# One fused attention-and-FFN layer on one core: setup chunks 0 to 2 reordered on VectorE, TensorE and ScalarE, one high part moved to GpSimd, and the row transpose of x1 done as two transfers

## The reference, cut to what matters

```python
r = sigmoid(x @ Wr); k = x @ Wk; v = x @ Wv
state = decayed running sum over time of k * v     # per channel
y = rmsnorm(r * state, ln_w)
x = layernorm(x + y @ Wo)
h = gelu(x @ (alpha1 * sign(w1)).T + b1)           # 256 -> 1024
x = layernorm(x + h @ (alpha2 * sign(w2)).T + b2)  # 1024 -> 256
```

## Time and profile before

| | us |
|---|---|
| median of 3 runs (822.38 to 822.54) | 822.49 |
| the profiled execution | 822.86 |
| its span | 821.0 |
| TensorE products, busy | 798.2 (97%) |
| VectorE, busy | 772.6 (94%) |
| ScalarE, busy | 678.9 (83%) |
| GpSimd, busy | 295.6 (36%) |

### The profile page before, as it was taken

The page is one execution under the profiler, slowest core; times in us unless marked ns, Lnnn a source line. Parts: engine busy times, 40 slices in busy tenths (PEclk is TensorE's granted clock), DMA queues, the critical chain, the costliest instruction groups (busy, mean ns, idle before and its releaser), DMA issues.

```text
span 821.0 us, 16564 instructions
## 1 busy us (share of the span) xinstructions
PE 798.2 (97%) x5173; PEld 505.3 (62%) x5173; DVE 772.6 (94%) x1467; ACT 678.9 (83%) x971; POOL 295.6 (36%) x570
## 2 busy tenths in 40 slices
PE   6989999999999999999999999999999999999986
PEld 4555666656666656666656666665666665666653
DVE  7998999999999999999999999999999999999886
ACT  7887888888888888888888888888888888887775
POOL 3343323344323344233344333344332334332344
PEclk9999999999999999999999999999999999999999
DMA  8413554444553434554434554444455344444313
GB/s 249 91 46 78 129 113 94 102 103 102 128 128 83 110 88 102 128 128 92 113 80 109 118 128 103 102 90 108 109 128 112 93 98 106 102 102 103 78 33 97
DMA packets 169847, 86.27 MB, mean 105 GB/s; under 512 B 130145, under 2 KB 165473, under 8 KB 169825
## 3 DMA queue, kind: packets, MB, share of 16 engines
q1 hardware_dynamic: 148304, 52.97, 29.8%
q0 software_dynamic: 4608, 16.78, 10.8%
q10 hardware_dynamic: 16912, 16.26, 5.8%
HBM read 20.45 MB, written 16.78 MB: 45 GB/s over the span
## 4 chain that ended last, share of the span: by engine, by line
PE 89%; DVE 4%; POOL 2%; issue 2%; ACT 2%; DMA 1%; POOLq 0%; DVEq 0%; ACTq 0%; SPq 0%
PE ps_r L362 28%; PE ps_o L483 26%; PE ps_f L433 19%; PE ps_r L433 6%; PE ps_o L388 6%; PE ps_o L393 3%; DVE hid_lo L981 1%; DMA x_in<-in_L_attn_x_dram 1%; DVE u L932 1%; ACT hid L662 1%; DVE u_st L940 0%; PE ps_s L370 0%; POOL root L1284 0%; POOL y_sqs L1272 0%; ACT hid_hi L697 0%
## 5 line engine op out<-in xcount | busy, mean ns | idle before, releaser
L483 PE MATMUL ps_o<-w2T,hid_hi 128*128 128x256 f16 x992 | 218.9, 273 | 3.4 <-DVE hid_lo L981 3.0
L483 PE MATMUL ps_o<-w2T,hid_lo 128*128 128x256 f16 x992 | 218.8, 273 | 0.0
L362 PE MATMUL ps_r<-x_t,proj_hi 128*128 128x512 f16 x768 | 197.1, 379 | 1.7 <-DVE proj_lo L1057 1.2
L433 PE MATMUL ps_f<-x_t,w1T 128*128 128x512 f16 x768 | 181.7, 379 | 1.6 <-DVE x_t L965 1.3
L662 ACT ACTIVATE hid<-ps_f,b1c,f_scale 128x512 f32<-128x512 f32 x192 | 145.3, 774 | 41.6 <-PE ps_f L433 36.6
L981 DVE SCALAR_TENSOR_TENSOR hid_lo<-hid,hid_scale,hid_hi 128x1024 f16<-128x1024 f32 (+1 forms) x136 | 160.3, 1222 | 0.9 <-POOL hid_hi L1305 0.6
L1272 POOL TENSOR_TENSOR y_sqs<-y_sq 128x512 f32<-128x512 f32 x32 | 46.7, 1459 | 308.4 <-ACT y_sq L637 308.4
L362 PEld LDWEIGHTS ps_r<-x_t,proj_hi 128*128 128x128 f16 x768 | 74.5, 98 | 92.1 <-issue 3.4
L697 ACT ACTIVATE hid_hi<-hid,hid_scale 128x2048 f16<-128x2048 f32 (+2 forms) x72 | 128.0, 1778 | 3.2
L433 PEld LDWEIGHTS ps_f<-x_t,w1T 128*128 128x128 f16 x768 | 74.9, 98 | 79.6 <-issue 1.6
L362 PE MATMUL ps_r<-x_t,proj_lo 128*128 128x512 f16 x384 | 114.2, 379 | 0.0
(11 more groups left out here) (182 smaller groups left out, 1333.0 us busy)
## 6 DMA issues: line engine op xcount, KB each, us to landing
x_in<-in_L_attn_x_dram SPq DMA_DIRECT2D x32, 512.0 KB, 4.4
res<-b_row POOLq DMA_DIRECT2D x32, 512.0 KB, 4.6
out_dram<-res ACTq DMA_DIRECT2D x31, 512.0 KB, 3.1
w_in<-in_L_ffn_w_dram SPq DMA_DIRECT2D x2, 1024.0 KB, 10.2
x_t<-x_st SPq DMA_TRANSPOSE x59, 4.3
b_row<-in_L_ffn_b_dram SPq DMA_DIRECT2D x1, 512.0 KB, 13.2
proj_in<-in_L_attn_Wk_dram SPq DMA_DIRECT2D x1, 256.0 KB, 5.2
proj_in<-in_L_attn_Wv_dram SPq DMA_DIRECT2D x1, 256.0 KB, 5.4
```

The source lines that it names most:

```text
L362: last = nc.tensor.matmul(ps_r[:, m, :], w[:, m, dc, ec * P:(ec + 1) * P], xx[:, :, dc, :], start=(n == 0), stop=(n == 3 * DC - 1))
L433: last = nc.tensor.matmul(f1_bank[hc % NF], w1T[:, hc, dc, :], xx[:, :, dc, :], start=(dc == 0 and n == 0), stop=(dc == DC - 1 and n == 1))
L483: last = nc.tensor.matmul(o_tok[:, tt, :], hh[:, hc, tt * P:(tt + 1) * P], w2T[:, :, hc, :], start=(hc == 0 and n == 0), stop=(hc == HC - ...
```

## The change

- TensorE's prologue: T1(0) stands behind R(2)'s group ec=1, m=0 instead of m=1. F1(0) of tile 0 stands ahead of sum_wmax, which now also waits for take_bounds(1,3).
- VectorE's prologue: x1l(0) ahead of hidden_bound; block_sums(1) ahead of hidden_scale; scans(2,2,0) behind mean_sq(1); hl of pairs 0 and 1 behind ustats(1), then norm1(1), hl of pairs 2 and 3, x1l_rows(1), kvs(2,2,1), scans(2,2,1).
- ScalarE's prologue: alphas2 in two parts, one after the second r gate of chunk 2 (ahead of gelu of tile 0), the other after gelu of tile 2; the high part of pair 1 is left out; that of pair 3 ahead of x1h_rows(1).
- GpSimd: the high part of pair 1 (`hh_first`), the product that scales alpha2 (within `diagonal`), and the order unscales, diagonal, hh_first, root_u(1), x1b(0).
- SyncE: x1's transpose in every chunk is two transfers, the high half after x1h_rows and F1, the low half after x1l_rows. The semaphore x1t counts 32 instead of 16 for a chunk.

```diff
@@ sync
-            sp.sem_inc(s_x1t, 16)
+            sp.sem_inc(s_x1t, 32)
...
-            def transpose(dst, src):
-                return sp.dma_start(dst[:, :, :, :, :].rearrange("p s tt dc t -> p (s tt dc) t"),
-                                    src[:, :, :, :].rearrange("p s tt d -> p (s tt d)"), transpose=True)
+            def transpose(dst, src, parts=slice(0, 2)):
+                return sp.dma_start(dst[:, parts].rearrange("p s tt dc t -> p (s tt dc) t"),
+                                    src[:, parts].rearrange("p s tt d -> p (s tt d)"), transpose=True)
...
-                    sp.wait_ge(s_x1l, i + 2)
+                    sp.wait_ge(s_x1h, i + 2)
                     sp.wait_ge(s_f1, HC * i + HC)
                     sp.sem_inc(s_issued, 1)
-                    transpose(x1_t, x1_st).then_inc(s_x1t, 16)
+                    transpose(x1_t, x1_st, slice(0, 1)).then_inc(s_x1t, 16)
+                    sp.wait_ge(s_x1l, i + 2)
+                    sp.sem_inc(s_issued, 1)
+                    transpose(x1_t, x1_st, slice(1, 2)).then_inc(s_x1t, 16)
@@ tensor
-                    pe.wait_ge(s_x1t, 16 * c + 16)
+                    pe.wait_ge(s_x1t, 32 * c + 32)
...
-                R(2, False, looped=False, ecs=(1,), slot=2, ms=range(2))
+                R(2, False, looped=False, ecs=(1,), slot=2, ms=(0,))
                 T1(0, 0, True)
-                R(2, False, looped=False, ecs=(1,), slot=2, ms=(2,))
+                R(2, False, looped=False, ecs=(1,), slot=2, ms=range(1, 3))
                 pe.wait_ge(s_ms, 1)
-                sum_wmax(ps_wmax[:, 5:6], 5, 1, 6)
                 sum_bounds(1, NCH)
                 pe.wait_ge(s_w1T, 16)
-                F1(0, NCH, range(0, 3), gates=3)
+                F1(0, NCH, range(0, 1), gates=3)
+                pe.wait_ge(s_xtmp, 4)
+                sum_wmax(ps_wmax[:, 5:6], 5, 1, 6)
+                F1(0, NCH, range(1, 3), gates=3)
@@ scalar
-                act.wait_ge(s_x1t, 16 * c)
+                act.wait_ge(s_x1t, 32 * c)
...
-            def hh(c, part):
+            def hh(c, part, counted=0):
...
-                                     scale=hid_scale[:, :]).then_inc(s_hh, part.stop - part.start)
+                                     scale=hid_scale[:, :]).then_inc(s_hh, part.stop - part.start + counted)
...
                 r_gates(2, 2, (0,))
-                act.wait_ge(s_sgn2, 1)
-                alphas2()
                 x1h(0, 1)
                 ysq(1, (1,), y=y_second)
                 r_gates(2, 2, (1,))
+                alphas2((0,))
                 act.wait_ge(s_ready, 1)
                 gelu(0, range(0, 1))
                 yh(1, y_second)
                 gelu(0, range(1, 2))
                 act.wait_ge(s_ready, 2)
                 hh(0, pairs[0])
-                gelu(0, range(2, 4))
-                hh(0, pairs[1])
-                gelu(0, range(4, 6))
-                hh(0, pairs[2])
+                gelu(0, range(2, 3))
+                alphas2((1,))
+                gelu(0, range(3, 6))
+                hh(0, pairs[2], counted=2)
                 gelu(0, range(6, 8))
+                hh(0, pairs[3])
                 x1h_rows(1, 1)
-                hh(0, pairs[3])
                 xh_rows(3, 3)
@@ vector
-                if first:
+                if first and part.start == 2:
+                    dve.wait_ge(s_hh_pool, 1)
+                elif first:
                     dve.wait_ge(s_hh, part.stop)
...
-                dve.wait_ge(s_alpha, HC + DC)
-                nc.vector.tensor_scalar(alpha2[:, :], alpha2[:, :], w_max[:, 5:6], 1.0 / (H * HTOP), ALU.mult,
-                                        ALU.mult).then_inc(s_hidden, 1)
...
+                x1l(0)
                 hidden_bound()
-                x1l(0)
                 take_bounds(1, 3)
+                block_sums(1)
                 hidden_scale()
-                scans(2, 2, 0)
-                block_sums(1)
                 yl(1, y_second)
                 mean_sq(1)
-                hl(0, pairs[0], first=True)
+                scans(2, 2, 0)
                 residual1(1, 1)
                 ustats(1)
+                hl(0, pairs[0], first=True)
+                hl(0, pairs[1], first=True)
+                norm1(1, 0, 1)
+                hl(0, pairs[2], first=True)
+                hl(0, pairs[3], first=True)
+                x1l_rows(1, 1)
                 kvs(2, 2, 1)
-                norm1(1, 0, 1)
-                hl(0, pairs[1], first=True)
-                hl(0, pairs[2], first=True)
-                x1l_rows(1, 1)
-                hl(0, pairs[3], first=True)
                 scans(2, 2, 1)
@@ gpsimd
+            def hh_first(part):
+
+                pool.wait_ge(s_gelu, part.stop)
+                pool.wait_ge(s_ready, 2)
+                nc.gpsimd.tensor_scalar(hid_hi[:, part, :], hid[:, part, :], hid_scale[:, :], 1.0, ALU.mult,
+                                        ALU.mult).then_inc(s_hh_pool, 1)
+
             def diagonal():
 
-                pool.wait_ge(s_hidden, 1)
+                pool.wait_ge(s_alpha, HC + DC)
+                pool.wait_ge(s_hread, 1)
+                nc.gpsimd.tensor_scalar(alpha2[:, :], alpha2[:, :], w_max[:, 5:6], 1.0 / (H * HTOP), ALU.mult,
+                                        ALU.mult).then_inc(s_alpha2, 1)
+                pool.wait_ge(s_alpha2, 1)
...
                 scales(3, 3)
-                diagonal()
                 root_rms(1)
                 unscales(3, 3)
+                diagonal()
+                hh_first(pairs[1])
+                root_u(1, True)
                 pool.wait_ge(s_b2_in, 16)
                 x1b(0, 0)
-                root_u(1, True)
```

More of the change, by code:

```diff
@@ L215, in postln_layer_kernel @@
         s_diag, s_arow = sem("diag_s"), sem("arow_s")
-        s_hidden, s_hread, s_row = sem("hidden_s"), sem("hidden_read_s"), sem("alpha2_row_s")
+        s_hread, s_row = sem("hidden_read_s"), sem("alpha2_row_s")
         s_xsq, s_xroot = sem("xsq_s"), sem("xroot_s")
@@ L219, in postln_layer_kernel @@
         s_zlast = sem("zlast_s")
+        s_alpha2, s_hh_pool = sem("alpha2_s"), sem("hh_pool_s")
         s_uneg, s_ushift = sem("uneg_s"), sem("ushift_s")
@@ L742, in alphas1, with alphas2 @@
                                          accum_out=alpha1[:, hc:hc + 1]).then_inc(s_alpha, 1)
-            def alphas2():
+            def alphas2(dcs):
                 act.wait_ge(s_w2_in, 16)
-                for dc in range(DC):
+                act.wait_ge(s_sgn2, 1)
+                for dc in dcs:
                     nc.scalar.activation(w2_in[:, dc, :], w2_in[:, dc, :], ACT.Abs,
```

## The result

The changed kernel takes 824.19 us (median of 20 runs, 822.66 to 825.69); beside it on the same chip the kernel before took 822.53 (20 runs, 822.31 to 822.67). The ratio is 1.0019, 95% interval 1.0013 to 1.0025: 1.7 us slower where 1.8 us faster was forecast, and above the range. The ratio is just under the 0.2% from which the prediction counts a difference; its interval, though, lies wholly above 1. The 20 times lie in three groups, 822.66 to 823.22 (7), 824.14 to 824.28 (9) and 825.57 to 825.69 (4); those of the kernel before lie in one. The profiled execution took 824.28 us, span 822.5, so it belongs to the middle group.

The account below looks back on a forecast made before the run. TensorE was taken as the bound, full from 93 to 773 us, with 4.24 us of setup holes to win. Second products 1.91 us earlier less a 0.1 stall gave 1.8: 822.49 to 820.7 us, range 820.1 to 821.9.

Parts of the forecast that it names:

- T1's place: TensorE's prologue: T1 one product group earlier, ending near 42.8 instead of 43.87.
- F1's start: TensorE's prologue: F1 starts at 45.6, after the last two groups of R(2) end at 45.32.
- the low products of O(1): TensorE's prologue, chunk 1: they go at 50.28 instead of 50.81, once `yl` is written at 50.22.
- the products that wait for nothing at 57.7: Chunk 0's second products on TensorE: after fillers and alpha row, pair 0's start at 57.7 without a wait.
- the half transpose's 3.1 us: x1's transpose before F1(1): a half lands in 3.1 us, a whole in 4.3; TensorE stalls about 0.1 us.
- step 1: Prologue, VectorE and GpSimd: the root is hidden, nothing holds residual1 or `hl`; fourth low part at 61.97, 1.91 us earlier.
- step 2: GpSimd's prologue: `x1b`, issued near 58.3 instead of 53.53, is read only at 70, so hidden.
- B: Rival, x1's transpose: half takes as long as a whole; stall 1.2 us, gain 0.7, time 821.8; chance 0.15.
- D: Rival, every chunk: two transposes don't overlap; 1.8 us lost 29 times, 873 us; chance 0.04.
- C: Rival, GpSimd's prologue: slow at its new work, high part 2.40, norm1 1.1 us late, 821.8; chance 0.07.
- E: Rival, loop's first turn: VectorE is the bound; chunk 2's bounds and `yl(2)` late, half the gain returned, 821.6; chance 0.06.
- X: Theory formed after the measurement, not forecast: `x1b`'s 512 KB, moved next to x1's transposes, slows their landing.

Follow-up runs that it names:

- experiment 7: The changed kernel with `kvs(2,2,1)` between `ustats(1)` and the first `hl`, not behind `x1l_rows`: 823.78 us, 1.001 of the kernel before.
- experiment 8: experiment 6 with `kvs(2,2,1)` in place of `scans(2,2,0)` behind `mean_sq(1)`, both scans at the end: 821.85 us, 0.9992 of the kernel before.
- experiment 5: The changed kernel with `x1b(0)` issued at 53.80, ahead of `diagonal`, instead of 61.14: 823.87 us, 1.0013 of the kernel before.
- experiment 1: The changed kernel again without edit, profiled in its slowest group: 824.32 us, 1.002 of the kernel before.
- experiment 4: The changed kernel with 25 idle products instead of 8 ahead of the second products: 824.84 us, 1.0028 of the kernel before.
- experiment 9: The kernel before with `x1b(0)` alone moved, behind `root_u(1)` and x1's high half (issued 61.08): 823.44 us, 1.0019 of the kernel before.
- experiment 6: experiment 5 with the 17 more idle products of experiment 4: 822.76 us, 1.0002 of the kernel before.
- experiment 3: The kernel before with only x1's transpose split into two transfers: 821.88 us, 0.9993 of the kernel before.
- experiment 10: experiment 8 with `x1b(0)` ahead of `root_rms(1)`, in GpSimd's idle time (issued 48.55): 821.21 us, 0.9985 of the kernel before.
- experiment 11: experiment 10 without the 17 extra idle products (8 as before): 821.98 us, 0.9993 of the kernel before.

## Why the prediction was wrong

**What held.** T1's place, F1's start, `yh`, the low products of O(1), the 1.11 us high part on GpSimd (1.4 taken), the products that wait for nothing at 57.7, and the half transpose's 3.1 us where nothing disturbs it. (The prediction's estimate of 3.0 us from the Trainium skill's page "DMA: Bandwidth & Descriptors" is near it, although the section Anatomy of one DMA states the fixed part of 2.0 us for transfers that GpSimd issues, and the transposes are SyncE's.) The loop is full, and the bounds of chunk 2 didn't become late. VectorE idled 0.95 instead of 1.5 ahead of `yl`, because `hid_bound` took 1.07 instead of 0.16 beside GpSimd's `y_sqs` (1.27 from 45.02); that this cost nothing is luck, idle time swallowed it.

**Failed step 1: "root_u(1) ... takes 1.6 with its 1.03 root, and is wanted at 58.17 ... All hidden", and residual1 and `hl` where nothing "holds" them.** root_u(1) took 3.05 us (56.63 to 59.68), and the root of the mean square 1.93 instead of 1.03. Along VectorE's list the delays add up: scan started 0.09 late, 0.49 more at residual1, 0.95 more at `norm1`, so that the fourth low part was written at 63.49 and not at 61.97. Of the 1.91 us that the new order was to win, 0.38 was left (products at 63.55 against 63.93). I took a duration from a row and not the neighbour with it. The prediction looked for neighbours of the *high part* and named scan and `hl` as the operations to fear; both had been moved beside the two roots, and that was not weighed. (`yl`, `x1l_rows` and y also read two SBUF tensors, so its "only the scan and `hl`" is too narrow.) The trace of the kernel before had rows with the new neighbour: near its end `u_ve` and `u_rstd` stand beside six `hl` of 512 columns (788.72 to 792.75), on GpSimd

```profile
788.99 0.49 POOL L1293 TENSOR_SCALAR u_ve<-u_mv 128x4 f32<-128x4 f32 x1 [2.37 <-DVE u_mv L944]
789.57 1.40 POOL L1295 TENSOR_TENSOR u_rstd<-u_ve,neg_half 128x4 f32<-128x4 f32 x1
```

They take 0.3 and 0.4 us more than in the loop, beside VectorE operations half as long.

The mechanism as the runs show it: a GpSimd operation of 4 columns beside a VectorE operation with two inputs in SBUF (`hl` of 1024 columns, scan of 512) takes 0.8 to 1.0 us more; beside `kvs` it doesn't (experiments 7 and 8). The Trainium skill's page "SBUF — State Buffer" (Who interferes with whom) has this rule: the two engines share one pair of ports under an exclusive lock, and VectorE takes it for its second SBUF input when GpSimd reads SBUF. Here the trace agrees, with 0.19 against 1.02 us, and both ways round (`hl` 2.45 to 3.07 beside the high part). So semaphores are not the only thing that ties these two engines together.

The neighbour isn't all: the operation that starts second is the one that is held. In the kernel before, the root started 0.19 ahead of an `hl` and took no longer than in the loop; `rms` started within that `hl` and took 0.44, to 0.07 behind its end, where it takes 0.20 in the changed kernel:

```profile
51.31 1.28 DVE L981 SCALAR_TENSOR_TENSOR hid_lo<-hid,hid_scale,hid_hi 128x1024 f16<-128x1024 f32 x1 [0.28 <-ACT hid_hi L697]
```

```profile
51.12 1.02 POOL L1284 TENSOR_TENSOR root<-ms,neg_half 128x4 f32<-128x4 f32 x1 [1.57 <-DVE ms L922]
52.22 0.44 POOL L1287 TENSOR_TENSOR rms<-root,y_inv 128x4 f32<-128x4 f32 x1
```

In the changed kernel the scan starts at 50.52, ahead of the root at 50.69, and `hl` at 56.35, ahead of `u_ve` at 56.63. The other way round, `y_sqs` and the high part of experiment 5 start first and keep their 1.27 and 1.11, and `hid_bound` and `hl` are late. No run changes only the order of the starts.

**Failed step 2: "`x1b`, now issued near 58.3 instead of 53.53, is read at 70".** That its reader is late enough is true, and it is not the price. Its 512 KB move at the same time as the transposes, whose halves land in 5.1 to 6.7 us (experiments 1 and 4) instead of 3.1. It was issued at 61.14, and not at 58.3, because step 1 had delayed GpSimd. In its forecast place it would, by estimate, have cost nothing: from the prediction's own times (norm1 through at 59.5, some 1.1 for `x1h_rows`, 0.2 to the issue) the high half goes out near 60.8, 2.5 behind x1b, and at that distance the low half landed in 3.1 in experiment 7. So step 2 is a lack of margin that step 1 used up. The prediction reckoned with the new place of a DMA as the time at which its data is wanted, not as load on the transfer engines; the DMA share of 1.17 during a transpose was quoted, and says that they are busy throughout. That the place of x1b decides is shown: experiment 9 gives 1.0 us for it alone, experiments 5 and 6 take the slow landing away. That the cause is the shared transfer engines is argued from their share (1.03 while both were under way).

**Missing altogether: the clock.** The prediction counted the holes of the setup as time only. Behind the 2.45 us hole TensorE ran at 1.2 GHz for 3.4 us, worth 1.6 us where nothing hides it; experiments 5 and 6 differ by 1.1 us by it. The longest hole in the second products of the kernel before was 1.28 us:

```profile
63.93 0.28 PE L483 MATMUL ps_o<-w2T,hid_hi 128*128 128x256 f16 x1 [1.28 <-DVE hid_lo L981]
```

The new order put one of 2.45 there, between the second and the third low part. By the prediction's own times, an estimate, it would have been some 1.2 us (pair 1's products through at 59.6, the third low part written at 60.8). So this hole, too, grew from step 1: most of its other 1.2 us is the 0.91 that `norm1` waits for the root.

**The rivals.** B and D fall by experiment 3. C had the right symptom, `norm1` waiting for GpSimd, and put it to the high part at 2.40; it was 1.11. C's rule was at hand and was weighed for the wrong operation. E didn't occur. None of the five was X or the clock.

**What stays open.** How an execution of the fastest group (822.7) spends its time: by span (1.5 less) F1(1) would start near 69.15 there, so the low half would have landed in some 4.1 us; this is arithmetic, not seen. And the tail: 0.85 us in the profiles, of which up to 0.37 may belong to the profiled execution of before (822.86, median 822.49); the rest goes with the split, cause unknown. What decides whether the clock falls is open as well.

## What to carry to other kernels

When work is moved on one engine, write down the new *neighbours* of every small operation on the others, above all GpSimd's beside VectorE operations with two SBUF inputs: take its duration from a row with the same neighbour that started in the same order, or expect a microsecond more. The order may change with any shift of tenths. A moved DMA is priced by what it flies beside, not only by when its data is read. And a hole ahead of a block of products can cost twice, as idle time and by the clock of what follows. Here times in groups went with it (what decides whether the clock falls stays open), and 17 idle products took the groups away for 0.3 us (experiments 10 and 11).

## What the hardware did that was not expected

- A 4-column GpSimd operation went from 0.19 to 1.02 us, its root from 1.01 to 1.93, by a neighbour that had started first.
- Two transposes of 256 KB issued 2.1 us apart each landed in 3.1; with a 512 KB transfer of GpSimd's queue issued 1.2 us ahead of them they took 5.1 to 6.7, with one 2.5 us ahead 3.7 and 3.1.
- Of the two profiled executions of the changed kernel, the clock fell in one behind the hole of 2.45 us in the second products. In the other it stayed full behind that hole (2.44) and fell behind the next, of 2.09 (experiment 1). The groups of experiments 7 and 11 suggest that it also fell behind holes of about 1.4 and 1.8 us, and in experiment 6 none came behind 1.44. So the length of the hole alone doesn't set it.
